# Graph attention layer pair on one core: five products as native fp32 matmuls in place of three rounded ones, with a second buffer for x^T

## The reference, cut to what matters

```
v = relu(x @ Wv + bv);  q = relu(x @ Wq + bq);  k = relu(x @ Wk + bk)
att = softmax(where(mask, q @ k.T, -9e15))          # 1024 x 1024 for each graph
x1  = layernorm(x + relu((att @ v) @ Wo + bo))
h   = x1 @ Ww.T + Wb;  e = h @ a1;  f = h @ a2
u   = mask * exp(e[:, None] + f[None, :] + ab);  a = u / sum(u)
out = layernorm(x1 + a @ h)
```

## Time and profile before

| | |
|---|---|
| time, median of 3 runs | 398.25 us (398.11 to 398.5) |
| span of the profiled execution | 397.6 us (what the measured time has around it: 0.65 us) |
| busy: PE, DVE, ACT, POOL | 382.8, 345.1, 331.2, 280.4 us |
| instructions | 8890, of them 2769 matmul records |

### The profile page before, as it was taken

The page is one execution under the profiler, slowest core; times in us unless marked ns, Lnnn a source line. Parts: engine busy times, 40 slices in busy tenths (PEclk is TensorE's granted clock), DMA queues, the critical chain, the costliest instruction groups (busy, mean ns, idle before and its releaser), DMA issues.

```text
span 397.6 us, 8890 instructions
## 1 busy us (share of the span) xinstructions
PE 382.8 (96%) x2769; PEld 356.5 (90%) x2769; DVE 345.1 (87%) x1056; ACT 331.2 (83%) x661; POOL 280.4 (71%) x258
## 2 busy tenths in 40 slices
PE   8899999999999999999999999999999999999990
PEld 7699988999999999999999998999999999999990
DVE  4887898899779998899969998799988999898976
ACT  5678678997789888898879978898888969999962
POOL 1454862597538995689937999289966799486673
PEclk9999999999999999999999999999999999999997
DMA  7917515836568077663596365870766647968011
GB/s 253 342 43 266 164 65 179 310 122 239 179 219 317 13 281 230 237 249 131 182 298 250 149 235 172 284 296 22 265 202 211 277 157 260 397 220 279 17 55 53
DMA packets 38157, 80.72 MB, mean 203 GB/s; under 512 B 2784, under 2 KB 19680, under 8 KB 38112
## 3 DMA queue, kind: packets, MB, share of 16 engines
q1 hardware_dynamic: 37824, 80.03, 57.7%
q10 hardware_dynamic: 288, 0.14, 0.2%
HBM read 75.96 MB, written 4.19 MB: 202 GB/s over the span
## 4 chain that ended last, share of the span: by engine, by line
PE 87%; DVE 6%; issue 3%; DMA 2%; POOL 1%; SPq 0%; POOLq 0%; DVEq 0%
PE m_ps L1775 14%; PE pt_ps L1727 13%; PE s_ps L1651 7%; PE av_ps L1739 7%; PE av_ps L1741 7%; PE av_ps L1740 7%; PE s_ps L1653 7%; PE s_ps L1652 7%; PE m_ps L1658 6%; PE m_ps L1659 3%; PE m_ps L1651 2%; PE m_ps L1653 2%; PE m_ps L1652 2%; PE m_ps L1756 2%; DMA raw<-in_adj_dram 2%
## 5 line engine op out<-in xcount | busy, mean ns | idle before, releaser
L1041 DVE TENSOR_TENSOR prob_tl<-pt_ps,prob_th 128x512 fp32r<-128x512 f32 x128 | 85.5, 681 | 6.2 <-ACT prob_th L672 6.0
L672 ACT ACTIVATE prob_th<-pt_ps 128x512 fp32r<-128x512 f32 x128 | 74.7, 596 | 18.6 <-PE pt_ps L1727 18.5
L1033 DVE CUSTOM_DVE_ANT_0 prob<-s_ps,penalty 128x1024 f32<-128x1024 f32 x64 | 77.9, 1217 | 10.8 <-PE s_ps L1653 6.6
L404 POOL TENSOR_SCALAR penalty<-raw 128x1024 bf16<-128x1024 f32 x64 | 66.6, 1049 | 26.8 <-DMA raw<-in_adj_dram 13.0
L664 ACT ACTIVATE prob<-prob,neg_max 128x1024 f32<-128x1024 f32 x64 | 73.7, 1152 | 1.9 <-DVE neg_max L1033 1.9
L1727 PE MATMUL pt_ps<-rhs,prob 128*128 128x128 f32 x512 | 73.9, 274 | 0.0
L1739 PE MATMUL av_ps<-prob_th,vh 128*128 128x256 f32 x256 | 73.6, 288 | 0.0
L1741 PE MATMUL av_ps<-prob_th,vl 128*128 128x256 f32 x256 | 72.3, 282 | 0.0
L1740 PE MATMUL av_ps<-prob_tl,vh 128*128 128x256 f32 x256 | 72.3, 282 | 0.0
L606 ACT ACTIVATE adj_t<-adjt_in 128x1024 fp32r<-128x1024 f32 x56 | 59.3, 1062 | 11.2 <-PE m_ps L1775 11.2
L1775 PE MATMUL m_ps<-g,adj_t 128*128 128x258 f32 x448 | 63.1, 287 | 0.4
(11 more groups left out here) (161 smaller groups left out, 918.4 us busy)
## 6 DMA issues: line engine op xcount, KB each, us to landing
raw<-in_adj_dram SPq DMA_DIRECT2D x64, 512.0 KB, 5.6
adjt_in<-in_adj_t_dram SPq DMA_DIRECT2D x56, 512.0 KB, 4.0
x_in<-in_x_dram SPq DMA_DIRECT2D x8, 512.0 KB, 7.0
raw<-in_adj_t_dram SPq DMA_DIRECT2D x8, 512.0 KB, 5.7
raw<-in_x_t_dram SPq DMA_DIRECT2D x15, 256.0 KB, 4.4
out_dram<-out_sb SPq DMA_DIRECT2D x14, 256.0 KB, 4.1
out_dram<-out_sb SPq DMA_DIRECT2D x4, 128.0 KB, 1.8
wb<-in_pack_b_dram SPq DMA_DIRECT2D x1, 320.0 KB, 5.2
```

The source lines that it names most:

```text
L672: sc.activation(prob_th[n % 2][:, tiles(k), (i % 2) * P:(i % 2 + 1) * P], pt_ps[k][:, :].rearrange("p (c n) -> p c n", n=P), ACT.Copy).the ...
L1033: v.tensor_tensor_reduce(out=prob[i % 2][:, :], in0=s_ps[:, :, :].rearrange("p a n -> p (a n)"), in1=penalty[:, n % RING, :], scale=-1.0, ...
L1041: v.tensor_tensor(prob_tl[n % 2][at], pt_ps[k][:, :].rearrange("p (c n) -> p c n", n=P), prob_th[n % 2][at].bitcast(F32), ALU.subtract).th ...
```

## The change

- **q, k, v, o, h** are single native fp32 matmuls: `pe.matmul(q, w_q, x)`, x^T and the weights as loaded, in fp32. `product_side_by_side` and the splits of x, of the weights, of av and of x1^T are gone (`x_hi`, `x_lo`, `split_in`, `split_vo`, `av_lo`, `x1_lo`, half of `split_w1`).
- **What empties them** has one step less: `v_bias` adds in place (no `v_sum`), `o_out` scales and adds in one (no `o_bias`, `o_sum`), `h_out` copies two tiles at once in place of eight reduces. Two tiles of h share a bank, so four slots of `h` stand where eight stood.
- **x^T** has two buffers. The load of batch b waits until PE has read batch b - 2, and PE waits for the load itself.
- The order of what remains is as it was, with `h` by pairs of tiles.

```diff
@@ SyncE
+            def rows_read(b, k):
+                for read in (q_full, k_full):
+                    sp.wait_ge(read, 2 * b + k + 1)
+                sp.wait_ge(v_full, TH * b + 2 * k + 2)
...
             def load_x_t(b, k):
-                if b > 0:
-                    sp.wait_ge(*lower(xtl_done, b - 1, k))
-                sp.dma_start(half(xt_in, k), half(x_t[b], k)).then_inc(xt_arrived[k], 16)
+                if b > 1:
+                    rows_read(b - 2, k)
+                sp.dma_start(half(xt_in[b % 2], k), half(x_t[b], k)).then_inc(xt_arrived[b % 2][k], 16)
@@ GpSimd: x_lo gone.  ScalarE
-            def x_hi(b, k):
-                for read in (q_full, k_full):
-                    wait(act, read, 2 * (b - 1) + k + 1)
-                wait(act, v_full, TH * (b - 1) + 2 * k + 2)
-                act.wait_ge(xt_arrived[k], 16 * (b + 1))
-                sc.activation(half(xth, k), half(xt_in, k), ACT.Copy).then_inc(xth_done, 1)
-            def av_hi(b, n):
+            def av_out(b, n):
-                sc.activation(avh[:, n * PAIR:(n + 1) * PAIR], av_ps[:, 0:PAIR], ACT.Copy).then_inc(avh_done, 1)
+                sc.activation(av[:, n * PAIR:(n + 1) * PAIR], av_ps[:, 0:PAIR], ACT.Copy).then_inc(av_done, 1)
@@ VectorE
-                v.tensor_tensor(v_low[j % 2][:, :, :], vv[:, :, 1, :], rows(bv_row, 2), ALU.add).then_inc(v_biased, 1)
-            def v_sum(b, j):
...
+                v.tensor_tensor(vv, vv, rows(bv_row, 2), ALU.add).then_inc(v_biased, 1)
-            def av_lo(b, n):
-            def x1_lo(b, k):
-            def o_sum(b, j):
...
-            def h_out(b, t):
-                v.tensor_reduce(h_sb[:, t, :], bank["h", b, t][:, 0:2 * E1].rearrange("p (a e) -> p e a", a=2),
-                                AX_X, ALU.add).then_inc(h_done, 1)
+            def h_out(b, u):
+                v.tensor_copy(h_sb[:, pair(u), :], bank["h", b, u][:, 0:2 * E1].rearrange("p (t e) -> p t e", e=E1)).then_inc(h_done, 1)
@@ TensorE
+            def rows_here(b, k):
+                if b == 0 and k == 0:
+                    pe.wait_ge(xt_quarter, 16)
+                pe.wait_ge(xt_arrived[b % 2][k], 16 * (b // 2 + 1))
...
             def project_q(b, k):
-                pe.wait_ge(*lower(xtl_done, b, k))
+                rows_here(b, k)
                 q = shared("q", b, k)
-                product(q[:, :], (wqh, wql), (half(xth, k), half(xtl, k))).then_inc(q_full, 1)
+                pe.matmul(q[:, :], w_q, half(xt_in[b % 2], k), start=True, stop=True).then_inc(q_full, 1)
             def project_v(b, j):
                 for c in range(2):
-                    last = product_side_by_side(vv[:, c * PAIR:(c + 1) * PAIR], (blk(xth, t), blk(xtl, t)), flat(w_hl[:, 2, :, :]), D)
+                    last = pe.matmul(blk(vv, c), blk(xt_in[b % 2], 2 * j + c), w_v, start=True, stop=True)
-            def project_h(b, t):
+            def project_h(b, u):
-                product_side_by_side(hh[:, 0:2 * E1], (blk(x1th, t), blk(x1tl, t)), flat(w1hl[:, :, :]), E1).then_inc(h_full, 1)
+                for c in range(2):
+                    last = pe.matmul(hh[:, c * E1:(c + 1) * E1], blk(x1t, 2 * u + c), w1[:, :], start=True, stop=True)
```

More of the change, by code:

```diff
@@ L69, in resnorm_kernel @@
         adjt_last = sb("adjt_last", [P, T, T, P], F32R)
-        xt_in, qf, kf, vf = (raw[:, j, :] for j in range(4))
+        xt_even, qf, kf, vf = (raw[:, j, :] for j in range(4))
+        xt_in = [xt_even, sb("xt_odd", [P, N])]
         adj_in = raw[:, RING:2 * RING, :]
@@ L405, in convert @@
                                  ALU.mult, ALU.add).then_inc(penalty_done, 1)
-            def x_lo(b, k):
-                pool.wait_ge(xth_done, 2 * b + k + 1)
-                gp.tensor_tensor(half(xtl, k), half(xt_in, k), half(xth, k).bitcast(F32), ALU.subtract).then_inc(xtl_done[1], 1)
             def q_hi(b, k):
@@ L684, in norm0, with x1t_out @@
                                   scale=rstd0[:, j:j + 1]).then_inc(x1_done, 1)
-            def x1_hi(b, k):
-                wait(act, h_full, T * (b - 1) + TH * (k + 1))
+            def x1t_out(b, k):
+                wait(act, h_full, TH * (b - 1) + 2 * (k + 1))
                 act.wait_ge(x1t_full, 2 * b + k + 1)
-                sc.activation(half(x1th, k), bank["x1t", b, k][:, :], ACT.Copy).then_inc(x1th_done, 1)
+                sc.activation(half(x1t, k), bank["x1t", b, k][:, :], ACT.Copy).then_inc(x1t_done, 1)
             def exp_ef(b, k):
@@ L779, in head @@
                 q_out(0, 1)
-                x_hi(1, 0)
                 v_relu(0, 0)
@@ L1432, in batch_pass @@
                 mask_max(p, 6)
-                h_out(p - 1, 2)
-                h_out(p - 1, 3)
-                x1_lo(p - 1, 1)
+                h_out(p - 1, 1)
                 prob_lo(p, 4, 1)
@@ L1744, in project_out @@
             def project_out(b, j):
-                pe.wait_ge(avl_done, TH * b + j + 1)
+                pe.wait_ge(av_done, TH * b + j + 1)
                 o = shared("o", b, j)
                 for c in range(2):
-                    t = 2 * j + c
-                    last = product_side_by_side(o[:, c * PAIR:(c + 1) * PAIR], (blk(avh, t), blk(avl, t)), flat(w_hl[:, 3, :, :]), D)
+                    last = pe.matmul(blk(o, c), blk(av, 2 * j + c), w_o, start=True, stop=True)
                 last.then_inc(o_full, 1)
@@ L1777, in aggregate @@
                 last.then_inc(agg_full, 1)
-            def project_out_pair(j):
-                pe.wait_ge(avl_done, TH * LAST + j + 1)
-                o = shared("o", LAST, j)
-                for c in range(2):
-                    t = 2 * j + c
-                    last = product(blk(o, c), (blk(avh, t), blk(avl, t)), (woh, wol))
-                last.then_inc(o_full, 1)
             def transpose_x1_pair(j):
@@ L1795, in project_h_pair @@
             def project_h_pair(u):
-                pe.wait_ge(x1tl_done, 2 * LAST + u + 1)
+                pe.wait_ge(x1t_done, 2 * LAST + u + 1)
                 hh = shared("h_last", LAST, u)
                 for c in range(2):
-                    t = 2 * u + c
-                    last = product(hh[:, c * E1:(c + 1) * E1], (blk(x1th, t), blk(x1tl, t)), (w1h, w1l))
+                    last = pe.matmul(hh[:, c * E1:(c + 1) * E1], blk(x1t, 2 * u + c), w1[:, :], start=True, stop=True)
                 last.then_inc(h_full, 1)
```

355 lines of the change are left out of this document (104 added, 251 removed), and 6 rows, old and new, of the table PASS_SLOTS.

## The result

The changed kernel takes **400.47 us** (median of 6 runs, 400.05 to 400.86), the kernel before 398.18 in the runs beside it: ratio 1.0055 (1.004 to 1.007), 2.3 us slower. The profiled execution has a span of 398.7. The prediction said 398.1, range 396.4 to 400.4.

What follows compares the result with a forecast made beforehand. The prediction took PE's own instruction stream as the bound. Its terms, 4.2 + 0.5 - 1.2 - 1.2 - 1.2 - 1.2 = -0.1 on a span of 397.6, plus 0.65 outside it, gave 398.1 us, range 396.4 to 400.4.

Steps and rivals of the forecast that it cites:

- What a native matmul costs: q and k: native records of 512 columns take 0.43 us each, adding 28 x 0.15 = +4.2 us in batches 1 to 7.
- Rival 1: project_q and project_k: native records cost more than their steps, as fp32r ones do; slower, up to 400.6 us; 28%.
- rival 3: q and k: a native record streams a column in one step; -10.9 us, time 387; 4%.
- Waits on DVE in the passes: Five passes: PE's 0.25 us wait for a bank that agg_out empties goes; -1.2 us, from 0 to -1.3.
- v, o, h: Pairs of tiles, 35 times 0.04 us more where transposes follow, slightly less elsewhere: +0.5 us, from 0 to +1.4.
- The mask in batch 1: Scores in batch 1 stop waiting 0.98 us for DVE's mask; with a small avl wait -1.2 us, from -0.5 to -1.5.
- The head: Start of the kernel: second tile of scores at some 14.7 in place of 15.9; -1.2 us, from -0.5 to -1.7.
- The last o and h: Near the end: six pairs of tiles get shorter and the avl wait goes; -1.2 us, from 0 to -1.5.
- The sum: Whole kernel: 4.2 + 0.5 - 1.2 - 1.2 - 1.2 - 1.2 = -0.1 on a span of 397.6, giving 397.5 us.
- The runs lie 0.65 above the span: Time outside the span: 0.65 us added to the predicted span of 397.5 to give 398.1 us.

Runs made afterwards that it cites:

- qk_native_alone: The kernel before with only q and k native and the second buffer for x^T; v, o and h stay split: 401.89 us, ratio 1.0083.
- qk_split: The changed kernel with q and k again as three fp32r products each, x_hi, x_lo and their split weights back: 394.92 us, ratio 0.992.
- before_again: The kernel before, unchanged, run again for a second trace: 398.49 us, span 396.7.
- tail_order: The changed kernel with g_lo_pair(0) and o_out(LAST, 3) moved ahead of the previous batch's statistics in DVE's order at the end: 400.64 us, ratio 1.006.
- after_again: The changed kernel, unchanged, run again for a second trace: 399.99 us, ratio 1.005.
- both_again: The changed kernel with a one-column activation first on ACT and POOL's second conversion held until DVE has both kl of batch 0: 398.93 us, ratio 1.002.

## Why the prediction was wrong, step by step

- **What a native matmul costs: right.** 0.43 between records of 512 columns as predicted. 28 x 0.15 = 4.2 us were to be added; from the second tile of scores of batch 0 to the third of batch 7, which holds all 28 halves, qk_native_alone takes 3.2 and 3.5 us more than the two traces of the kernel before, and the changed kernel 4.0 more than qk_split. Rival 1 (overhead as in fp32r) and rival 3 (one step a column) fall. By the Trainium skill, "FP8 and Floating Point Precision", section TensorE Precision Notes, a true fp32 product is four passes; for 512 columns the trace comes near it, with 2 x 0.43 against 0.23 for one fp32r record, 3.7 times. The Trainium skill's rule in "TensorE: Matmul & The Clock Gate", section Back-to-back issue gap, would give 0.216 for a record: half of what is measured.
- **Waits on DVE in the passes, and v, o, h: right in the net.** The prediction had +3.0 for 20 halves, +0.36 for v, o and h and -1.2 for the waits, 2.2 in five passes; measured +1.99 against the trace that it read (236.46 against 234.47) and +1.68 against before_again, whose one long batch makes the 0.3 between. By halves it is less close: the kernel with v, o and h alone native takes 1.5 and 1.8 less than these two traces where -0.84 was predicted, and native q and k then cost 3.47 on top where 3.0 was.
- **The mask in batch 1: right in the gain.** The fifth tile of scores of batch 1 starts without the wait; from batch 1's start to its sixth tile the changed kernel makes up 0.94 us on before_again, with the longer q and k of that stretch inside.
- **The head: wrong, by 1.7 to 1.8 us.** "So scores start at some 14.7 in place of 15.9: -1.2 us". They start at 15.35, 15.22 and 15.28 (tail_order), and the kernel before starts them at 14.75, when the rows of batch 1 do not come late. 1.1 of it is that the 15.89 held one execution's late transfer, taken for the kernel's. The other 0.5 to 0.7 is what the removed steps had done on the side, which ate what was left of the gain: x_hi had drawn the table load forward and x_lo had held POOL's second conversion back from DVE. The prediction costed both at nothing, since they "lie beside 46.54 us of PE in each 46.60"; that is a figure of the middle of the kernel, and in the head they cost 1.03 and 0.31 us (after_again against both_again). Put right, they give 1.1 to 1.4 us of the time back. The predicted cost of the first q, "at doubled time 4 x 0.43", holds in after_again and both_again and not in the first trace.
- **The last o and h: wrong, by 1.0 us.** "I take -1.2 us, from 0 (the g chain binds at once)". It bound at once: from the last tile of scores to the first aggregation of the last batch the changed kernel takes 23.97 us, before_again 23.92. The prediction had ACT's exp, scale and copy in that chain and x1_lo as its relief; the runs show it is DVE's queue, with the statistics of the batch before in it, and once these are moved, POOL's steps beside DVE's. Over the whole end 0.15 to 0.2 us were gained.
- **The sum.** Against before_again: +0.60 to the second tile of scores, +0.56 in the rest of batch 0 (four native halves), -0.77 in batch 1 and the start of batch 2, +1.7 in five passes, -0.15 from there to the end: +1.9, the ends at 396.7 and 398.7. The prediction's sum was -0.1 on 397.6; with its head and tail terms at what they measured (+0.6, -0.2) it would have been +2.7, so the rest of its terms erred by 0.8 to the other side.
- **"The runs lie 0.65 above the span": wrong.** It is 1.7 to 1.9 in every run of every kernel; the two errors, 1.15 too little outside and a span 1.2 too long, cancelled for the kernel before and hid that the traced execution was a long one.

What stays open: why the transfer of the rows of batch 1 lands up to 1.1 us apart in executions of one kernel, why the first adjacency rows come at 8.2 in one trace and at 9.6 in another, when PE goes to its higher level in the head, and how the times vary with these; three traces of this head and two of the kernel before are few. The split of the 1.1 to 1.4 us between table load and conversion rests on one pair of traces. The second buffer by itself was not tried.

## What to carry to other kernels

Price a replaced product by its steps and neighbours, but list for every instruction that is taken away what it did on the side: whether it was its engine's first (it draws the table load) and whether it kept a neighbour from running beside someone else's critical step. Before a gain is booked in a wait near the start, check that wait against a second execution; and book a gain at the end only on the engine that has room there. Here the best version was half of the change: native v, o and h, where a product is 128 columns and the other engines are relieved, and split q and k, where a product is 512 columns and native costs 0.13 to 0.17 us more for each: 394.9 us, 0.8% below the kernel before.

## What the runs showed of the hardware

- **fp32 at 512 columns:** two records 0.43 us apart, at a granted clock of 1.00; at 128 columns 0.112. 512 columns as fp32r take 0.23.
- **The function table:** 1.28 us, placed directly ahead of ACT's first activation and behind its wait. An activation of one column (0.20 us) at the start moves it to 1.71.
- **POOL beside DVE:** a DVE subtraction of 128 x 512 takes 0.68 to 0.69 us alone. Ten times in eight traces one starts while POOL converts 128 x 1024, and each time it ends 0.53 to 0.54 us after POOL's end, whatever its start: it takes 1.00 to 1.52. The other way round, a conversion (1.05 alone) that starts in such a subtraction ends 0.90 to 0.91 after DVE's end, five times in three traces, and takes 1.15 to 1.51. So the later one waits for the other rather than running slower beside it. DVE's `den` and `shift` of 128 x 2 waited the same way for POOL's norm1 (above), while its reduces from PSUM beside the same steps kept their 0.42. The Trainium skill, "Trainium Architecture — The Big Picture", section What this means for kernel authors, has the port that DVE and GpSimd share as an exclusive lock; the trace agrees.
- **Time outside the span:** 1.7 to 1.9 us for all the kernels here.
